# A decoder block with a top-2 expert layer: the rows of an expert slot fetched in 32-row bands and turned by VectorE instead of TensorE

## The reference, cut to what matters

```
x = layernorm(x + retention(x))            # decay mask, group norm over the sequence
x = layernorm(x + attention(x, context))   # causal, 16 heads
x = layernorm(x + experts(x))
```

```
probs = softmax(xf @ router_w.T)                       # [4096, 8]
topk_probs, topk_idx = top_k(probs, 2); normalised
h   = gelu(einsum('nc,ech->neh', xf, w_fc) + b_fc)     # 256 -> 1024 per expert
out = einsum('neh,ehc->nec', h, w_proj) + b_proj       # 1024 -> 256 per expert
y   = einsum('nec,ne->nc', out, combine)               # only the two chosen experts count
```

## Time and profile before

| | |
|---|---|
| Runs | 985.74, 986.08, 988.63 us |
| Profiled execution, first to last instruction | 984.6 us |
| TensorE busy | 923.6 us (94%) |
| VectorE busy | 663.6 us (67%) |
| ScalarE busy | 607.6 us (62%) |
| GpSimd busy | 381.9 us (39%) |
| Mean granted TensorE clock | 0.979 |
| All DMA, mean | 81 GB/s |

### The profile page before, as it was taken

How to read it: one execution, slowest core, us unless ns; L and a number is a source line. 1 busy time by engine, 2 the same in 40 slices (tenths; PEclk the granted TensorE clock), 3 DMA queues, 4 the chain that set the end, 5 groups by cost and what they waited for, 6 DMA issues and landing times.

```text
span 984.6 us, 29858 instructions
## 1 busy us (share of the span) xinstructions
PE 923.6 (94%) x10845; PEld 821.1 (83%) x10845; DVE 663.6 (67%) x1977; ACT 607.6 (62%) x1531; POOL 381.9 (39%) x639
## 2 busy tenths in 40 slices
PE   6899999999999999999987999999999999999950
PEld 4788888888888888888777999999999999999950
DVE  4577787777877877877744677575755775665536
ACT  4556656656556666666556566576765675665536
POOL 0224554555544656555524422222222223222223
PEclk9999999999999999999989999999999999999985
DMA  8111141111111111113012552523434433523228
GB/s 280 50 34 57 61 142 45 56 56 66 56 46 44 63 59 61 51 54 110 29 34 50 120 139 44 139 45 67 120 57 130 100 83 57 131 43 48 43 48 325
DMA packets 57361, 79.90 MB, mean 81 GB/s; under 512 B 5728, under 2 KB 46048, under 8 KB 57120
## 3 DMA queue, kind: packets, MB, share of 16 engines
q1 hardware_dynamic: 41504, 58.50, 18.1%
q0 software_dynamic: 13536, 18.16, 10.6%
q10 hardware_dynamic: 2208, 1.73, 0.6%
HBM read 52.10 MB, written 29.71 MB: 83 GB/s over the span
## 4 chain that ended last, share of the span: by engine, by line
PE 79%; ACT 7%; DVE 5%; issue 4%; DMA 2%; SPq 1%; POOL 1%; ACTq 0%; another core or an unknown queue 0%; DVEq 0%; POOLq 0%
PE bank L828 16%; PE bank L842 11%; PE bank L511 11%; PE bank L844 5%; PE bank L647 4%; PE bank L673 4%; PE bank L573 3%; PE bank L718 3%; PE bank L694 3%; PE bank L626 3%; PE bank L598 3%; PE bank L593 2%; ACT h_f L1171 2%; PE bank L732 2%; ACT last_out L1243 1%
## 5 line engine op out<-in xcount | busy, mean ns | idle before, releaser
L828 PE MATMUL bank<-xs_hi,w_both 128*128 128x256 f32 x1152 | 242.2, 287 | 1.3 <-DVE xs_lo L1471 0.8
L1165 ACT ACTIVATE h_parts<-bank,bfc_s 128x256 fp32r<-128x256 f32 x288 | 139.9, 486 | 154.6 <-PE bank L828 150.5
L1721 POOL DMA_INDIRECT residual_sum<-y_w,meta_i x72 | 114.6, 1591 | 299.6 <-DVE y_w L1543 275.7
L1501 DVE TENSOR_TENSOR h_parts<-h_f,h_parts 128x256 fp32r<-128x256 f32 x288 | 121.4, 426 | 140.2 <-ACT h_f L1171 136.6
L842 PE MATMUL bank<-w_both,h_parts 128*128 128x512 f32 x544 | 200.0, 398 | 1.1 <-DVE h_parts L1501 1.1
L828 PEld LDWEIGHTS bank<-xs_hi,w_both 128*128 128x128 f32 x1152 | 191.5, 190 | 9.4 <-issue 1.6
L828 PE MATMUL bank<-xs_lo,w_both 128*128 128x256 f32 x576 | 162.9, 283 | 0.0
L844 PE MATMUL bank<-w_both,h_parts 128*128 128x256 f32 x544 | 153.1, 281 | 0.0
L1171 ACT ACTIVATE h_f<-bank,bfc_s 128x256 f32<-128x256 f32 x288 | 139.4, 484 | 3.9 <-DVE h_parts L1501 3.4
L842 PEld LDWEIGHTS bank<-w_both,h_parts 128*128 128x128 f32 x544 | 102.5, 188 | 20.0 <-DVE h_parts L1501 4.0
L828 PEld LDWEIGHTS bank<-xs_lo,w_both 128*128 128x128 f32 x576 | 109.7, 191 | 0.0
(11 more groups left out here) (186 smaller groups left out, 2138.2 us busy)
## 6 DMA issues: line engine op xcount, KB each, us to landing
rows<-sent_rows SPq DMA_DIRECT2D x37, 258.0 KB
xc_raw<-in_turned SPq DMA_DIRECT2D x32, 256.0 KB, 3.0
w_raw<-in_w_fc SPq DMA_DIRECT2D x8, 1024.0 KB
w_raw<-in_w_proj SPq DMA_DIRECT2D x8, 1024.0 KB
x_t<-in_x SPq DMA_DIRECT2D x32, 128.0 KB, 2.2
residual_sum<-x_row SPq DMA_DIRECT2D x32, 128.0 KB, 1.7
last_in<-residual_sum SPq DMA_DIRECT2D x7, 512.0 KB, 7.8
result<-last_out SPq DMA_DIRECT2D x7, 512.0 KB, 2.7
```

Source lines behind the costliest of these rows:

```text
L828: last = mm(ps_h(g, j), w[:, at:at + P], v[:, k, :], start=(n == 0), stop=(n == 3 * NCH - 1))
L1165: A(h_hi[j % 4][:, :], ps_h(g, j), ACT.Gelu_apprx_tanh, bias=bias)
L1501: V.tensor_tensor(h_lo[j % 4][:, :], h_f[j % 2][:, :], h_hi[j % 4][:, :].bitcast(f32), ALU.subtract).then_inc(s["h_split"], 1)
L1721: G.indirect_dma_start(total, bass.IndirectOffsetOnAxis(meta_i[:, half:half + 1], 0), y_w[:, half, :], None, compute_op=ALU.add)\
```

## The change: what it does

The transposes leave TensorE. The fetch brings the rows in such an order that one VectorE instruction, which transposes each 32x32 block within its 32 partitions, gives channels on the partitions. For that the 256x256 block is fetched as eight transfers, one for each pair of a band of 32 partitions (q) and a half of the channels (k); each moves 256 pieces of 32 values (128 B). A ninth fetches the two extra columns (256 pieces of 8 B). VectorE turns the whole block in SBUF into `rows_c`, and `xs_high` and `split_rows` read that in place of the PSUM bank.

```diff
-        rows = sb("rows", [P, HALVES, ROW])
+        rows = sb("rows", [P, NCH * SLOT])
+        rows_meta = sb("rows_meta", [P, HALVES, 2])
+        rows_c = sb("rows_c", [P, NCH * SLOT])
...
+        bands = rows_c[:, :].rearrange("p (b k r) -> p k b r", k=NCH, r=TW)
...
+        FETCHED = 16 * (NT * NCH + 1)
...
+            def fetch(slot_rows_at):
+
+                for q in range(NT):
+                    band = rows[q * TW:(q + 1) * TW, :].rearrange("r (b k c) -> r b k c", k=NCH, c=TW)
+                    for k in range(NCH):
+                        at = k * P + q * TW
+                        sp.dma_start(band[:, :, k, :],
+                                     slot_rows_at[:, at:at + TW].rearrange("(b r) c -> r b c", r=TW))\
+                            .then_inc(s_rows, 16)
+                sp.dma_start(rows_meta[:, :, :], slot_rows_at[:, C:ROW].rearrange("(h p) c -> p h c", p=P))\
+                    .then_inc(s_rows, 16)
...
-                sp.dma_start(rows[:, :, :],
-                             sent[ds(e, 1), ds(at, SLOT), :].rearrange("e (h p) c -> p (e h) c", p=P))\
-                    .then_inc(s_rows, 16)
+                fetch(sent[ds(e, 1), ds(at, SLOT), :].rearrange("e n c -> (e n) c"))
...
-            def turn_rows(g):
-                pe.wait_ge(s_rows, 16 * (g + 1))
-                for k in range(NCH):
-                    for half in range(HALVES):
-                        last = tr(ps_xs(g)[:, k * SLOT + half * P:k * SLOT + (half + 1) * P],
-                                  rows[:, half, k * P:(k + 1) * P], ident)
-                last.then_inc(s["rows_turned"], 1)
...
-                A(xs_hi[:, :, :].rearrange("p k t -> p (k t)"), ps_xs(g)[:, :], ACT.Copy).then_inc(s["xs_chain"], 1)
+                A(by_band(xs_hi), bands, ACT.Copy).then_inc(s["xs_chain"], 1)
...
+                        turn_rows(0)
                         take_rows(0)
                         split_rows(0)
...
+            def turn_rows(g):
+
+                dve.wait_ge(s_rows, FETCHED * (g + 1))
+                V.transpose(rows_c[:, :], rows[:, :]).then_inc(s["rows_turned"], 1)
```

More of the change, by code:

```diff
@@ L256, in ps_h @@
             return bank[j % 4][:, 0:SLOT]
-        def ps_xs(g):
-            return ps_prep
         ps_sum = (bank_g, ps_y)
@@ L265, in two_sums, with by_band @@
             return not (isinstance(g, int) and g < 2)
+        bands = rows_c[:, :].rearrange("p (b k r) -> p k b r", k=NCH, r=TW)
+        def by_band(xs):
+            return xs[:, :, :].rearrange("p k (b r) -> p k b r", r=TW)
         def ps_out(g, half):
@@ L401, in early_rows @@
                     apart(sp)
-                sp.dma_start(rows[:, :, :],
-                             sent_flat[g * SLOT:(g + 1) * SLOT, :].rearrange("(h p) c -> p h c", p=P))\
-                    .then_inc(s_rows, 16)
+                fetch(sent_flat[g * SLOT:(g + 1) * SLOT, :])
             def step(k):
@@ L476, in _ @@
             sp.wait_ge(s["meta_ready"], n_all + EVER)
-            sp.dma_start(rows[:, :, :], sent[0, 0:SLOT, :].rearrange("(h p) c -> p h c", p=P)).then_inc(s_rows, 16)
+            fetch(sent[0, 0:SLOT, :])
             def rows_of(rows, b):
@@ L772, in step @@
                     pair_run(prep_k, (k + 1) // 2)
-                    if k == B - 1:
-                        pe.wait_ge(s["v_out"], B)
-                        pe.sem_inc(s["rows_turned"], EVER)
-                        turn_rows(0)
                     run(x1_turn, At(k - 1))
@@ L858, in slot @@
                         proj(g, j - 3, w_both[par])
-                    if j == 5:
-                        turn_rows(g + 1)
                     if beside:
@@ L866, in fc0 @@
                     pe.wait_ge(s["w_ready"], HC)
+                    pe.wait_ge(s["v_out"], B)
                     pe.wait_ge(s["xs_ready"], 1)
@@ L929, in drain @@
                 logits(At(B - 2))
-                pe.wait_ge(s["h_done"], HC + EVER)
-                turn_rows(1)
                 proj0(7)
@@ L1423, in step @@
                     if k == B - 1:
-                        for name in ("meta_ready", "h_split", "y_biased"):
+                        for name in ("meta_ready", "h_split", "y_biased", "rows_turned"):
                             dve.sem_inc(s[name], EVER)
+                        turn_rows(0)
                         take_rows(0)
@@ L1464, in take_rows @@
             def take_rows(g):
-                dve.wait_ge(s_rows, 16 * (g + 1))
-                V.tensor_copy(meta_next[:, :, :], rows[:, :, C:ROW]).then_inc(s["meta_ready"], 1)
+                dve.wait_ge(s_rows, FETCHED * (g + 1))
+                V.tensor_copy(meta_next[:, :, :], rows_meta[:, :, :]).then_inc(s["meta_ready"], 1)
+            def turn_rows(g):
+                dve.wait_ge(s_rows, FETCHED * (g + 1))
+                V.transpose(rows_c[:, :], rows[:, :]).then_inc(s["rows_turned"], 1)
             def split_rows(g):
                 dve.wait_ge(s["xs_chain"], g + 1)
-                V.tensor_tensor(xs_lo[:, :, :].rearrange("p k t -> p (k t)"), ps_xs(g)[:, :],
-                                xs_hi[:, :, :].bitcast(f32).rearrange("p k t -> p (k t)"), ALU.subtract)\
+                V.tensor_tensor(by_band(xs_lo), bands, by_band(xs_hi).bitcast(f32), ALU.subtract)\
                     .then_inc(s["xs_ready"], 1)
@@ L1508, in slot @@
                         gate_rows(g - 1)
+                    if j == 5:
+                        turn_rows(g + 1)
                     if j == HC - 1:
@@ L1600, in drain @@
                 lg_out(At(B - 2))
+                turn_rows(1)
                 split_rows(1)
```

## The result

The changed kernel takes 991.66 us (median of 14 runs), the kernel before 986.14 us beside it; the ratio is 1.0057, 95% interval 1.0045 to 1.0069. A second set of runs gave 991.12 against 985.32 us, 1.0061 (1.0045 to 1.0078). It is slower by 0.6% where I had forecast 0.7% faster. One of the 14 runs took 3005.24 us and is left out of the ratio; the other 13 lie between 988.24 and 993.53 us.

A forecast was written before the change was run, and what follows sets the result against it. The prediction took TensorE, busy for 94% of the span, to bound ordinary slots. Its terms, -12.6 + 1.4 + 3.1 + 0.2 + 0.4 + 0.6, gave -6.9 us and a forecast of 979.2 us, own range 976 to 983, overall 974 to 992.

The forecast's parts named there:

- Term 1: Slots bound by TensorE: without its row transposes, 28 slots each get 0.45 us shorter, -12.6 us.
- Term 2: VectorE's new transpose, taken as 0.65 us: free in ordinary slots, 0.2 us in each of 7 split slots, +1.4 us.
- Rival B: No change: the VectorE transpose costs 1.38 us, twice the assumed time, giving 986.2 us; chance 0.13.
- Terms 3 and 4: Step 31: ScalarE waits for VectorE's late turn, +3.1 us; start of slot 1: turn chained across VectorE and ScalarE, +0.2.
- Rival C: Faster than forecast: step 31's delay is absorbed by other slack, giving 976.1 us; chance 0.15.
- Term 5: Nine SyncE row transfers instead of one: rows in time in 25 slots, about 0.4 us late in slot 4, +0.4 us.
- F: The moment SyncE issues the first transfer of a slot's row fetch; landings and needs are counted from it.
- Term 6: Weight loads for experts 2 to 7, issued 3.7 us later behind the row transfers: 0.1 us in 6 slots, +0.6.
- Rival A: Slower: small pieces don't keep pace from 0.6 us per transfer, rows and weights late; 990.8 us or far above; chance 0.22.

The follow-up runs named there:

- four_turns: weights_early with four TensorE transposes of a constant, into a bank nothing reads, put back from slot 2 on; 993.19 us, ratio 1.0081.
- turn_twice: weights_early with a second VectorE transpose, into an unused tensor, ahead of each; 990.54 us, ratio 1.0057.
- before_pad: The kernel before with an unused 2 KB-a-partition tensor behind the row buffer, moving everything later in SBUF; 986.46 us, ratio 1.0011.
- before_nine: The kernel before, TensorE transposes kept, with rows fetched in eight transfers of 1 KB pieces plus one for the two columns; 1006.32 us, ratio 1.0209.
- after_again: The changed kernel, unaltered, run and profiled once more; 991.12 us, ratio 1.0061.
- weights_early: The changed kernel with the next expert's weights issued ahead of the nine row transfers, except for expert 1; 985.07 us, ratio 0.9997.
- half_waits: The changed kernel with a semaphore for each half of the weights, ScalarE waiting for the projection half only at its fifth piece; 982.49 us, ratio 0.9959.
- wide_bands: The changed kernel with channels dealt 64 to a band: five row transfers instead of nine, fc weights in four transfers; 985.99 us, ratio 1.0004.
- first_turn: The changed kernel with slot 0's and slot 1's turns earlier on VectorE and weights issued ahead of rows for every expert; 981.01 us, ratio 0.9957.
- wide_half_turn: The edits of half_turn on the five-transfer kernel of wide_bands; 973.80 us, ratio 0.9872.
- half_turn: The changed kernel with the edits of half_waits and turn_early together; 976.28 us, ratio 0.9894.
- turn_early: The changed kernel with slot 0's turn at the head of VectorE's step 31 and slot 1's ahead of the last logits; 987.16 us, ratio 1.0019.

## Why the prediction was wrong

The miss is 12.5 us: -6.9 forecast, +5.5 to +5.8 measured. By its own terms:

**Term 1 (TensorE's transposes go, -12.6) held.** From before to after, ordinary slots got 0.40 to 0.47 us shorter and the six behind later split slots 0.49 to 0.53. Over 27 of the 28 slots that is 12.1 us; slot 3 waits for its rows, and with 0.44 for it the sum is 12.6. Shown by the slots after, and by four_turns, which puts it back.

**Term 2 (transpose on VectorE, +1.4) was too high.** The size was right, 0.706 against 0.65, and with the weights in time the split slots take what they took before, 12.26 to 12.30: 0 in place of 0.2 each. Rival B falls with it: the transpose doesn't cost 1.38. A second transpose would, turn_twice shows, cost 0.37 a split slot; the slack there holds one. The Trainium skill's "Vector Engine (DVE) Microarchitecture Reference", The reshape front-end and per-opcode configuration, has one element per cycle and lane for a transpose; the trace agrees in so far as the transpose, 0.706 us, lasts within 2% as long as the subtraction of as many elements, 0.69.

**Terms 3 and 4 (step 31 and slot 1, +3.3) had the mechanism right and the size too high.** ScalarE stood for 4.25 us, forecast 4.1, and `att_p` began 3.5 us later than before, counted from the start of step 30, where I had 3.1. But I carried that to the end of the kernel undiminished, and the stretch behind it takes about half of it back. The distance from the start of step 30 (its first `ret_p` on VectorE) to the `xs_lo` of slot 1, in us, by the granted clock in the window 480 to 530 us:

| turn of slot 0 | clock 0.97 | clock 0.93 | clock 0.86 to 0.88 |
|---|---|---|---|
| on TensorE | before_pad 59.96, before_nine 59.95 | before 62.33 | |
| late on VectorE | | after 64.33, after_again 63.58, weights_early 64.21, four_turns 64.25 | half_waits 66.72, wide_bands 66.72 |
| early on VectorE | | first_turn 59.38, wide_half_turn 59.32 | half_turn 61.75, turn_early 61.88 |

At the clock of 0.93 the change costs 1.3 to 2.0 us here, not 3.3. The early turn gives back 4.2 to 5.0, which is more than was lost: it puts this stretch 3.0 us below the kernel before (slot 1 itself then takes 16.8 to 17.0 us, 0.3 to 0.8 more than with the late turn at that clock). So the 4.0 us of turn_early and the 6.2 by which half_turn lies below half_waits price the repair; they don't price the loss. Rival C, which had the 3.1 us absorbed, is right for about half of it, though not in its time. The two places of the turn weren't tried apart.

**Term 5 (the fetch, +0.4) failed in slots 3 and 4.** The nine had landed at F + 6.5 and F + 7.4 in the two profiles, not at 5.9 to 6.5: the interval is 0.48 us, not 0.46, and single issues take up to 1.65. They are far from the 18 us of the fixed cost paid in series: taking it as latency was right. The 2.0 us of the Trainium skill's "DMA: Bandwidth & Descriptors", Anatomy of one DMA, are moreover stated for transfers issued from GpSimd, and these are SyncE's. The fetch during slot 3, which is issued late, was thus 1.2 and 2.0 us late and not 0.4: slot 3 took 12.97 and 13.78 us where 11.73 was in reach. VectorE was idle for 2.8 and 3.6 us there. Then comes something that I had not thought of. The granted clock in slot 4, windows of that slot in after and in its second profile (columns: us, busy time and instructions of PE, PEld, DVE, ACT, POOL, then granted clock, DMA share, GB/s):

```profile
571.56:584.13 12.57, 12.24 (x84) 10.67 (x82) 11.13 (x27) 10.10 (x24) 4.43 (x2) 1.00 0.45 65
```

```profile
571.79:585.09 13.30, 13.30 (x84) 12.01 (x82) 11.16 (x28) 10.10 (x24) 3.92 (x2) 0.87 0.43 61
```

Slot 4 ran at 0.87 and took 13.2 to 13.4 us in after_again, weights_early, half_waits and half_turn, whose slot 3, with TensorE standing, took 13.5 to 14.2; it ran at 1.00 and took 12.4 to 12.7 in six others. But first_turn, turn_early and turn_twice kept 1.00 behind a slot 3 of 13.9, 13.7 and 13.6, and so did before_nine behind one of 17.93. So a stall may have a price after it is over; the profiles suggest it and don't show it. In all, half_turn to wide_half_turn is 2.5 us. In ordinary slots the term held: no wait but one of 0.5 us, in slot 32; behind a split the wait of 0.4 to 0.9 us was absorbed.

**Term 6 (the weights, +0.6) is the step that failed.** I had the weights land at F + 12.7 to 13.2 and need them at F + 13.1. The need was right (F + 13.2). They landed at F + 14.4. Of that, 0.1 to 0.2 us is the issue, F + 4.8 against F + 4.7; the rest is the way from the issue to the landing. The pages of before_pad, whose orders are those of before, and of after give it for the projection half (the last figure, us, median):

```profile
w_raw<-in_w_proj SPq DMA_DIRECT2D x8, 1024.0 KB, 7.8
```

```profile
w_raw<-in_w_proj SPq DMA_DIRECT2D x8, 1024.0 KB, 9.5
```

With an issue at F + 1.0, the landing before was thus at F + 8.8, and I had taken F + 8.0, the place where the rate leaves its plateau. That the tail of those rates is GpSimd's was read rightly. These are the queues of before in 754.4 to 757.0 us (packets, MB, share; the software queue is GpSimd's, the hardware queue SyncE's):

```profile
q0 software_dynamic: 254, 0.23, 56.2%
q1 hardware_dynamic: 35, 0.03, 3.5%
```

But the weights' last packets come within that tail, and the semaphore follows the last of them by 0.4 to 0.5 us in before_pad. The second error is the stretch: 9.5 for 7.8 is 1.7 us more, where I had allowed 1.0 for GpSimd's transfer. That transfer began 6.6 us or more behind the issue before; after, it begins 4.1 to 4.5 us behind it in the later split slots and all of it lies within the weights' stream, as here in 702.4 to 707.0 us:

```profile
q1 hardware_dynamic: 1330, 1.14, 75.8%
q0 software_dynamic: 288, 0.26, 35.6%
```

That this overlap makes up the whole 1.7 us is argued, not shown; before_nine, with 1 KB pieces, has the same 9.5, so it comes with the nine issues and not with small pieces. In sum it is F + 8.8, 3.9 more for the later issue and 1.7 more for the stretch, F + 14.4: some 1.1 us late, five times. In slot 6 ScalarE is ready 1.2 us sooner (F + 12.0) and the landing is later (F + 14.9 and F + 15.7 in the two profiles), 2.9 to 3.7 us late. The removal is worth 6.1 us for the five places and 8.6 to 10 for all six. A margin of -0.1 to +0.4 us priced at 0.1 was a bet on an instant that I could only bound; 1.2 us further on, the same sum has 6 places times 1.3.

**Rival A** named the right place, weights late in six slots and slots behind a split, and 990.8 us, near the result. Its mechanism was another: small pieces that don't keep pace from 0.6 us per transfer. They do keep pace: before_nine with 1 KB pieces is no earlier, and the interval stayed at 0.48 us. That its figure came so near is luck.

The terms as the runs price them, in us:

| term | forecast | shown | by |
|---|---|---|---|
| 1 | -12.6 | -12.6 (8.1 in four_turns, where late transfers stand) | slots, four_turns |
| 2 | +1.4 | 0 | split slots of half_waits |
| 3, 4 | +3.3 | +1.3 to +2.0 | step 30 to slot 1 at one clock |
| 5 | +0.4 | +2.2 to +2.5 | wide_half_turn |
| 6 | +0.6 | +8.6 to +10 | half_waits |
| sum | -6.9 | -0.5 to +1.9 | measured +5.5 to +5.8 |

The two figures of terms 5 and 6 are the difference of medians and that of the ratios to before. The terms take away the forecast gain, but 3.6 to 6.3 us of the measured loss stand in none of them, and their cause stays open. The placement in SBUF is between 0 and 2.2 us by before_pad. The granted clock is another candidate: its median is 0.979 in the 29 runs of before that stand beside after_again, and 0.973 in the six of after_again. In the window 480 to 530 us, five of the eleven profiles of changed kernels have 0.86 to 0.88, and the three with TensorE's turns have 0.93 to 0.97; by the table of terms 3 and 4, the lower clock is 2.4 to 3.1 us there. Whether the change brings that clock about or the spread does, three profiles on one side can't tell.

## What to carry to other kernels

Work taken off the busiest engine is worth only the slots that this engine ends; before counting it, list every wait that the replacement shifts. Give each the time of the semaphore's landing, not the end of the rate's plateau, and ask which other transfers the shift puts inside the stream. Where one queue issues a fetch and then a larger load, splitting the fetch into nine delays the load by eight issues; a consumer that waits for all of a load at its first piece turns that delay into a stall, and one more semaphore takes it away (8.6 us and more here). An operation moved to another engine must also find its place in that engine's order: the engine that follows it stands until its turn comes. And a repair can give more than the loss that it was made for, so what it gives is no price of that loss.

## What the runs showed of the hardware

SyncE's issues of small transfers come some 0.5 us apart whatever the pieces are (median over all fetches 0.50 us with 1 KB in before_nine, with 128 bytes in after and with 256 bytes in wide_bands). They slowed to 0.84 us on average (6.70 us for eight, once) right behind the issue of 2 MB. A VectorE transpose in 32 by 32 blocks of 128x512 fp32 within SBUF takes 0.70 to 0.71 us, about as long as a subtraction of that shape (0.69). Two loads of 1 MB issued one behind the other land 5.3 and 7.8 us behind their issues (before_pad), and 5.5 and 9.5 (after) where other transfers run among them.

The stretch from slot 0 to slot 1, where TensorE has gaps, repeats least of all, beside the slots that wait for a transfer. Windows 480 to 530 us of half_waits, half_turn and wide_half_turn (columns: us, busy time and instructions of PE, PEld, DVE, ACT, POOL, then granted clock, DMA share, GB/s):

```profile
480.00:530.00 50.00, 41.35 (x512) 33.95 (x510) 23.68 (x80) 29.04 (x67) 18.36 (x39) 0.86 0.14 36
```

```profile
480.00:530.00 50.00, 43.95 (x532) 36.86 (x531) 25.38 (x93) 31.66 (x71) 19.38 (x45) 0.86 0.16 38
```

```profile
480.00:530.00 50.00, 43.93 (x550) 37.25 (x548) 27.90 (x98) 34.00 (x77) 20.88 (x47) 0.93 0.15 41
```

The slot 0 to slot 1 distances are 46.18, 42.13 and 39.69 us: 4.0 us with the turn's place at one clock, and 2.4 with the clock at one place of the turn. Over 50 us a mean of 0.86 is 3.5 us less of full clock than 0.93. Kernels whose orders in this stretch are the same differ likewise: 43.04 to 43.79 us in after, after_again and weights_early at 0.93, 46.18 in half_waits at 0.86. One profiled execution can therefore be 2 to 3 us off in this stretch, which is why the prices above come from medians, from slots that repeat and from profiles at one clock.
